# Block 1 of the attention scores ends two pieces later in the feed-forward stream, with its drain and shifts inside a quantisation

## What is computed

```
xn   = layernorm(x)
rho  = w . tanh(text @ Ws + xn @ W + b)           # one tanh per row, token and feature
att  = softmax(rho over the 77 tokens, masked)
txt  = att @ text                                 # used only through two columns, Wcw and Wcb
x    = x + tanh(txt @ Wcw + bcw) * xn + tanh(txt @ Wcb + bcb)
hn   = fp4(layernorm(x))
h    = silu(hn @ fp4(w_gate).T) * (hn @ fp4(w_up).T)     # 1408 wide
out  = x + fp4(h) @ fp4(w_down).T
```

## Time and profile before

| what | us |
|---|---|
| median of three runs (lowest, highest) | 1538.8 (1537.33, 1539.91) |
| the profiled execution | 1539.24 |
| its span | 1537.4 |
| PE busy | 1432.1 (93%) |
| ACT busy | 1359.6 (88%) |
| DVE busy | 1157.2 (75%) |
| POOL busy | 248.7 (16%) |

### The profile page before, as it was taken

The page is one execution under the profiler, slowest core; times in us unless marked ns, Lnnn a source line. Parts: engine busy times, 40 slices in busy tenths (PEclk is TensorE's granted clock), DMA queues, the critical chain, the costliest instruction groups (busy, mean ns, idle before and its releaser), DMA issues.

```text
span 1537.4 us, 24122 instructions
## 1 busy us (share of the span) xinstructions
PE 1432.1 (93%) x9752; PEld 647.7 (42%) x9752; DVE 1157.2 (75%) x1783; ACT 1359.6 (88%) x1249; POOL 248.7 (16%) x389
## 2 busy tenths in 40 slices
PE   7988889856999999999999999989999999999998
PEld 4444444411333333334444444434444444555564
DVE  4699997944586666759666776698877787898887
ACT  5999989999999999999999999999999999433321
POOL 0122222200111010111011111011101111312211
PEclk9999999988999999999999999999999999999999
DMA  5133332320011111201111111112111111123332
GB/s 159 42 83 83 83 82 75 95 65 8 8 26 41 40 27 41 40 15 40 41 40 40 41 33 37 36 40 40 40 41 41 40 41 40 40 59 73 80 69 62
DMA packets 181557, 77.91 MB, mean 51 GB/s; under 512 B 163627, under 2 KB 165675, under 8 KB 181445
## 3 DMA queue, kind: packets, MB, share of 16 engines
q1 hardware_dynamic: 180224, 75.00, 21.0%
q10 hardware_dynamic: 1221, 1.36, 0.3%
HBM read 27.85 MB, written 8.39 MB: 24 GB/s over the span
## 4 chain that ended last, share of the span: by engine, by line
PE 52%; ACT 27%; DVE 17%; issue 2%; DMA 1%; POOL 1%; SPq 0%; ACTq 0%; DVEq 0%; POOLq 0%
PE rho L809 19%; ACT hring L628 17%; PE dn L906 10%; PE gu1g L892 5%; PE gu0g L892 5%; PE gu1u L892 5%; PE gu0u L892 5%; ACT hring L623 4%; DVE featT L985 2%; ACT wd_room L628 2%; DVE work L1019 2%; ACT featT L623 1%; ACT featT L628 1%; DVE work L1040 1%; DVE work L1039 1%
## 5 line engine op out<-in xcount | busy, mean ns | idle before, releaser
L628 ACT ACTIVATE hring<-featT,bias 128x1024 f32<-128x1024 f32 x688 | 729.2, 1156 | 2.6 <-PE rho L809 2.5
L809 PE MATMUL rho<-hring,wslide 128*32 128x512 f32 x3776 | 459.0, 611 | 61.5 <-ACT hring L628 52.4
L809 PEld LDWEIGHTS rho<-hring,wslide 128*32 128x32 f32 x3776 | 105.5, 111 | 338.6 <-issue 191.7
L628 ACT ACTIVATE featT<-featT,bias 128x1024 f32<-128x1024 f32 x220 | 236.3, 1178 | 2.2 <-PE rho L809 2.2
L906 PE MATMUL dn<-wd_room,turned 128*128 128x512 f16 x1023 | 230.6, 380 | 0.2 <-DMA turned<-work 0.2
L490 POOL TENSOR_SCALAR split_t<-sm 128x32 f32<-128x32 f32 (+4 forms) x82 | 19.7, 240 | 1178.1 <-DVE sm L1008 1178.1
L623 ACT ACTIVATE hring<-featT 128x4096 f32<-128x4096 f32 x57 | 207.5, 3640 | 0.4 <-DVE featT L985 0.4
L985 DVE TENSOR_SCALAR featT<-featT,bias 128x1024 f32<-128x1024 f32 x256 | 175.5, 750 | 11.9 <-ACT hring L623 7.6
L1309 DVE TENSOR_TENSOR work<-sg,gu1u 128x352 f32<-128x352 f32 x64 | 33.3, 521 | 173.9 <-ACT sg L661 173.1
L906 PEld LDWEIGHTS dn<-wd_room,turned 128*128 128x128 f16 x1023 | 96.4, 98 | 145.2 <-issue 36.0
L809 PE MATMUL rho<-featT,wslide 128*32 128x512 f32 x1056 | 126.4, 596 | 5.4 <-ACT featT L628 3.1
(11 more groups left out here) (228 smaller groups left out, 1578.5 us busy)
## 6 DMA issues: line engine op xcount, KB each, us to landing
xt<-in_x SPq DMA_DIRECT2D x32, 256.0 KB, 2.8
out<-xt SPq DMA_DIRECT2D x32, 256.0 KB, 2.3
work<-in_x SPq DMA_DIRECT2D x8, 512.0 KB, 4.1
xt<-in_x SPq DMA_DIRECT2D x6, 512.0 KB, 4.3
xt<-in_L_ffn_w_gate SPq DMA_DIRECT2D x11, 256.0 KB, 2.7
xt<-in_L_ffn_w_up SPq DMA_DIRECT2D x11, 256.0 KB, 3.0
work<-in_L_ffn_w_down SPq DMA_DIRECT2D x2, 704.0 KB, 5.1
xt<-in_L_ffn_w_down SPq DMA_DIRECT2D x2, 704.0 KB, 4.1
```

The costliest lines, as they stand in the source:

```text
L628: act.activation(slot[s][:, g, :], featT[:, e, ROW0[k]:ROW0[k] + rows], ACT.Tanh, bias=bias[:, e, base + tok:base + tok + 1]).then_inc(tan ...
L809: last = pe.matmul(rho[SLOTW * g:SLOTW * g + SLOTW, hf * 512:hf * 512 + 512], wslide[:, e, SLOTW - 1 - r:2 * SLOTW - 1 - r], slot[s][:, g, ...
```

## The change

`ENDS` replaces the fixed piece 2 as the last piece of a block: block 1 now ends behind piece (6, 4) (the first part of the down product of tile 5) and not behind piece (6, 2). Its 70 quads that lie in the stream are spread over 44 pieces in place of 42, and the 77 quads of block 2 over 54 in place of 56. Block 3 keeps its places. The turns of the drained scores follow piece (6, 5). ACT issues the quads up to number 156 ahead of the exps of block 1, then continues. On DVE, tile 6 gets a branch of its own: the rows of tile 7 come before the end of the block, the drain goes into the quantisation of the hidden rows (`between`), the two shifts behind its second step (`midway`), and the sums behind its end.

```
+    ENDS = [(0, -1), (BASE[1] - 2, 4), *((b - 2, 2) for b in BASE[2:])]
     for k in range(1, NBLK):
-        t0, p0 = (0, 0) if k == 1 else (BASE[k - 1] - 2, 3)
...
+        mine = [(t, p) for t in range(NT) for p in range(7)
+                if ENDS[k - 1] < (t, p) <= ENDS[k] and not (t == 0 and p >= 4)]
...
-                    if issued < QUADS:
+                    goal = 2 * QPB + 3 if SOFTMAX_AT[t] == 1 else min(issued + 1, QUADS)
+                    while issued < goal:
                         tanh_quad(issued)
                         issued += 1
...
-                    if t in SOFTMAX_AT and p == 3 and t < FREE_FROM:
+                    ended = t in SOFTMAX_AT and t < FREE_FROM and p == ENDS[SOFTMAX_AT[t]][1] + 1
+                    if ended:
                         softmax_transposes(SOFTMAX_AT[t], 0)
...
-                    hidden(t, 1, sums=begun is None)
-                if begun is not None and t != FREE_FROM:
+                    hidden(t, 1, sums=begun is None or begun == 1)
+                if begun == 1:
+                    rows_tile(t + 1)
+                    hidden(t, 2)
+                    hidden(t, 3)
+
+                    def shifts():
+                        softmax_shift(1, 0)
+                        softmax_shift(1, 1)
+
+                    quantise_hidden(t, between=lambda: softmax_drain(1), midway=shifts)
+                    softmax_sums(1)
+                elif begun is not None and t != FREE_FROM:
                     softmax_drain(begun)
```

More of the change, by code:

```diff
@@ L88, in bass_xattn_fp4_ffn @@
     score_from = {}
+    ENDS = [(0, -1), (BASE[1] - 2, 4), *((b - 2, 2) for b in BASE[2:])]
     for k in range(1, NBLK):
-        t0, p0 = (0, 0) if k == 1 else (BASE[k - 1] - 2, 3)
-        t1 = BASE[k] - 2
-        mine = [(t, p) for t in range(t0, t1 + 1) for p in range(7)
-                if (t, p) >= (t0, p0) and (t, p) <= (t1, 2) and not (t == 0 and p >= 4)]
+        mine = [(t, p) for t in range(NT) for p in range(7)
+                if ENDS[k - 1] < (t, p) <= ENDS[k] and not (t == 0 and p >= 4)]
         cost = [G_COST if p < 4 else D_COST for _, p in mine]
```

## The result

The changed kernel takes 1549.62 us (median of six runs, 1548.45 to 1551.35); the kernel before took 1538.89 beside it. The ratio is 1.0073, with an interval from 1.0062 to 1.0083: some 10.7 us slower. The prediction said 1539.5 us, at most 1542.8, so it was wrong. The profiled execution took 1549.44 us. The last quad's tanh ends at 1324.36 us (before 1314.10), and the span grew by 10.3 us, so the whole loss lies ahead of the feed-forward end.

The account below looks back on a forecast made before the run. The prediction took ACT to set the pace, so only its gaps counted: -0.37 + 0.3 + 0.2 + 0.6 = +0.7 us on the median of 1538.8 gave 1539.5 us, with a range from 1536.9 to 1542.8.

Parts of the forecast that it names:

- ACT sets the pace: From 382 us on ACT is the bound and PE follows through the ring; only gaps in ACT's list change the time.
- PE as the bound: Rival: PE bounds block 2, and 6.4 us of its work moves into idle time of block 1; 1532.4 us, chance 0.06.
- the late silu: Ahead of block 1's exps: the silu of piece (6, 3) no longer waits for PE, -0.37 us.
- two single-quad pieces more, at 0.3 each: Block 1: gate-and-up pieces followed by one quad stand three times, not once; +0.6 us, from 0 to 0.8.
- the same of them are summed by DVE: Whole stage: ACT's work does not change, since DVE sums the same quads as before; 0 us.
- the new end: End of block 1: exps do not wait, the gates wait about 0.3 us and the slot of quad 156 costs 0.2.
- PE's wait between the turns: End of block 1: PE waits 2.8 us for the shift before its second turn, before 1.27.
- the nine products behind the wait: End of block 1: the down product's third part, after PE's second turn, takes 2.0 us.
- the 0.3 us at the gates: End of block 1: DVE's sums end at 22.4, ACT wants the gates at 22.16; a new wait of about 0.3 us.
- the slot of quad 156: Behind two gate-and-up pieces after block 1's end: ACT and PE come level; 0.2 us, between 0 and 0.9.
- The clock's rival: New end of block 1: TensorE's clock falls behind PE's 2.8 us wait, costing 3.3 us; 1542.8 us, chance 0.03.
- The ring's rival: Block 1: the ring runs dry and ACT's slot waits grow at all eight narrow places; 1542.7 us, chance 0.11.

Follow-up runs that it names:

- a8_table: Changed kernel with block 1's quads laid by hand, two kept behind piece (1, 1), and the early sum of a7_early; 1540.89 us against 1538.75 for the kernel before.
- a9_hidden: Changed kernel with the hidden rows of piece (1, 0) multiplied inside tile 0's quantisation, not behind it; 1544.66 us against 1539.30 for the kernel before.
- a1_slot: Changed kernel with two quads again behind piece (1, 1) and one behind (1, 6); 1546.94 us against 1539.22 for the kernel before.
- a5_fill: Changed kernel with extra unread PE products, 32 ahead of piece (1, 2) and 26 between block 1's turns; 1546.42 us against 1538.75 for the kernel before.
- a3_order: Changed kernel with tile 6's summed quad of block 2 behind both shifts, not ahead of them; 1549.42 us against 1539.22 for the kernel before.
- a4_all: Changed kernel with the edits of a1_slot, a2_sums and a3_order together; 1542.91 us against 1539.22 for the kernel before.
- a7_early: Changed kernel with tile 6's summed quad of block 2 ahead of the drain, not behind it; 1548.35 us against 1538.75 for the kernel before.
- a2_sums: Changed kernel with DVE allowed to sum one quad further ahead inside tile 5's quantisation; 1547.37 us against 1539.22 for the kernel before.
- b1_slot: Kernel before with one quad moved from behind piece (1, 1) to behind (1, 6); 1544.37 us against 1538.75 for the kernel before.

## Why the prediction was wrong

**Right: ACT sets the pace, and its gaps count one to one.** ACT's busy time stayed, its gaps grew by 11.5 us, and the median by 10.7; a8_table speaks against PE as the bound.

**Right, and too small to matter: the late silu.** The 0.37 us ahead of the exps are gone. In the changed kernel the last quad's tanh ends at 677.72, and the three direct quads behind it follow without a gap.

**Wrong: two single-quad pieces more, at 0.3 each.** The step took a price worked out for a place where PE needs only slots of the ring. That price held at (6, 2), with 0.41 us, and at (1, 1) in a9_hidden, with 0.38; (2, 0) cost 0.71, and 1.5 in a1_slot. At (1, 1) it was 5.3 us, since PE there also needs a PSUM pair that DVE frees behind a quantisation; by a5_fill, 1.7 of them are the clock that falls behind this wait. The wait stood already in the trace of before, at 0.79 us in the timeline of PE; I read only ACT's waits there, where it was covered. A quad less on PE's list took that cover away.

**Wrong: "the same of them are summed by DVE", 0 us.** As many quads are summed, but not at the same point of DVE's list. The limit inside the quantisation, four quads beyond `before[t, 4]`, hangs on the table. With the new counts it excludes quad 146 by one: 2.67 us.

**Nearly right, and then priced wrong: the new end.** The drain's cover was predicted at 3.4 us and measured at 3.75, PE's wait between the turns at 2.8 and measured at 3.19, and the exps were not late. But the nine products behind the wait were priced at 2.0 us and took 4.04. So PE came late to the quads of block 2, and 1.77 us of ACT's time went there in place of the 0.3 us at the gates. At the slot of quad 156, priced at 0.2, it was 0.49. The gates did not wait, since ACT was late itself. a3_order shows that they do once ACT is on time.

**The rivals.** The clock's rival (0.03) happened, behind both waits. Its mechanism was right for the end of block 1, where by a5_fill it cost 2.3 us, and not 3.3; most of that was lost at the first quad of block 2 and not at quad 156. It did not foresee tile 1. I set it low on the strength of one row, the 2.83 us of the earlier trace rows without a fall. The Trainium skill ("TensorE: Matmul & The Clock Gate", section "Why this matters for your kernels") says that gaps of TensorE between bursts of matmuls put it back to the lower clock. The trace of the changed kernel agrees at both waits (3.92 and 3.19 us, then a granted clock of 0.86 and 0.66 around them), and a5_fill agrees by filling them (1.00 in both). The last section shows like waits with and without a fall. The ring's rival (0.11) had the right side and the wrong cause: slots account for some 4.2 us of waits, of which the longest, 1.42 us, stands behind the wait of tile 1.

So 5.3 (tile 1) + 2.8 (the sum) + 2.6 (the end of block 1) + 0.9 (tiles 2 to 5) = 11.6 us of gaps were priced at 0.7 in all. The step that failed first was not the new order at the block's end, on which most of the working was spent, but the table: it moved quads in all the tiles of two blocks, and I priced them by an average. The end of the block comes second: its wait was right, and the work behind the wait was priced at the upper clock.

## What to carry to other kernels

When one engine sets the pace, a table that is spread anew is to be followed at each place where its list meets an in-order step of another engine, not priced per piece: look for the waits of the *non-critical* engines that the old table just covered (0.79 us here), and for limits in the program that depend on the counts that changed. A wait of TensorE is to be priced twice, once as a wait and once at the lower clock for the work behind it, which may or may not come. And repairing one wait shows the next: of 1.77 us won at the turns, 1.10 came back at the gates.

## What the hardware did that was not expected

The clock fell behind a wait of TensorE in one kernel and stayed up behind a like wait in another. Behind the end of block 2 PE waits 2.83 us in the kernel before and in a4_all, and 2.82 in a8_table; between the two turns of block 2 it waits 1.27 us in the kernel before and in a7_early. The windows around these places (columns as in the earlier trace rows), first the kernel before:

```profile
999.00:1009.00 10.00, 8.73 (x61) 3.76 (x61) 8.17 (x17) 9.13 (x8) 1.92 (x4) 1.00 0.00 1
1028.00:1038.00 10.00, 7.07 (x52) 3.09 (x45) 9.01 (x26) 10.00 (x11) 0.00 (x0) 1.00 0.50 100
```

Then a4_all, a8_table and a7_early:

```profile
1030.50:1040.50 10.00, 7.17 (x46) 2.68 (x39) 9.01 (x26) 10.00 (x11) 0.00 (x0) 0.83 0.51 100
```

```profile
1028.00:1038.00 10.00, 7.18 (x44) 2.67 (x37) 9.01 (x27) 10.00 (x11) 0.00 (x0) 0.83 0.60 99
```

```profile
1008.00:1018.00 10.00, 8.73 (x54) 3.82 (x56) 8.19 (x17) 7.45 (x6) 1.89 (x4) 0.83 0.00 1
```

PE's list around each wait is the same, and the granted clock is 1.00 in the kernel before and 0.83 in the others. In a7_early the 12 products behind the turn took 4.44 us, and 2.75 before. Ten of the kernels have the wait behind the end of block 2, of 2.81 to 2.85 us: in five (before, after, a1_slot, a2_sums, a5_fill) the quad behind it took 1.92 or 1.93 us, in the other five (b1_slot, a3_order, a4_all, a8_table, a9_hidden) 2.42 to 3.25. So the length of the wait alone does not decide, and what does is open. Each kernel's clock was read from one profiled execution. Over whole executions it differs from run to run of the same kernel: the 13 of the kernel before beside a1_slot were granted 0.981 to 0.989. Where in them the clock fell is not on record.
